# Feed-forward phases token-major, with the hidden halves turned by DMA, squares summed on ScalarE and low halves on VectorE

## The reference, cut to what matters

```python
x = x + 0.5 * ffn(layernorm(x), w_up, w_down)
x = x + attn(layernorm(x), Wq, Wk, Wv, Wo)      # also sums each 16 tokens of layernorm(x)
x = x + 0.5 * ffn(layernorm(x), w_up, w_down)

def ternary_linear(x, w):
    alpha = mean(abs(w)); w_t = sign(w) * (abs(w) > 0.5 * alpha)
    return einsum('bsd,fd->bsf', x / (rms(x) + 1e-8), w_t)
ffn(x) = ternary_linear(gelu(ternary_linear(x, w_up)), w_down)    # 256 -> 1024 -> 256
```

## Time and profile before

| | us |
|---|---|
| median of 3 runs | 2338.8 (2338.52 to 2339.14) |
| the profiled execution's own time | 2342.05 |
| its span, first to last instruction | 2340.3 |
| first feed-forward phase, first statistics to last side sum | 43.8 to 404.8 |
| attention | 404.8 to 2047.3 |
| second feed-forward phase, first statistics to end | 2047.6 to 2340.3 |

### The profile page before, as it was taken

How to read it: one execution, slowest core, us unless ns; L and a number is a source line. 1 busy time by engine, 2 the same in 40 slices (tenths; PEclk the granted TensorE clock), 3 DMA queues, 4 the chain that set the end, 5 groups by cost and what they waited for, 6 DMA issues and landing times. The chain is left out here.

```text
span 2340.3 us, 79203 instructions
## 1 busy us (share of the span) xinstructions
PE 2110.0 (90%) x30563; PEld 1603.8 (69%) x30563; DVE 1992.6 (85%) x4704; ACT 2050.7 (88%) x4166; POOL 1628.5 (70%) x1453
## 2 busy tenths in 40 slices
PE   1888885799999999999999999999999999879998
PEld 0555554578777777777777777777777777646666
DVE  6799996798888888898988988988889989768785
ACT  2888894599999989999998999998999999789997
POOL 1677775477777767777776777777677777556765
PEclk9999998899999999999999999999999999989999
DMA  5200000499999989999998999999999999801011
GB/s 180 72 0 0 0 0 1 76 170 167 173 171 167 175 135 171 168 176 168 171 169 140 171 171 172 173 171 161 150 169 173 170 168 178 128 10 36 27 36 37
DMA packets 1076094, 289.57 MB, mean 124 GB/s; under 512 B 1056304, under 2 KB 1074736, under 8 KB 1075760
## 3 DMA queue, kind: packets, MB, share of 16 engines
q1 hardware_dynamic: 1075760, 285.02, 77.1%
HBM read 14.68 MB, written 8.39 MB: 10 GB/s over the span
## 5 line engine op out<-in xcount | busy, mean ns | idle before, releaser
L1010 POOL TENSOR_TENSOR probs_split<-probs,probs_split 128x512 f16<-128x512 f32 (+1 forms) x1026 | 1148.5, 1131 | 429.3 <-DVE probs_split L1347 298.2
L1336 DVE CUSTOM_DVE_ANT_0 probs<-score_ps,mask,neg_qk_scale 128x512 f32<-128x512 f32 (+1 forms) x1028 | 740.5, 721 | 97.2 <-PE score_ps L1114 95.4
L1275 ACT ACTIVATE probs<-probs,minus_max 128x512 f32<-128x512 f32 (+1 forms) x1027 | 718.6, 700 | 90.4 <-DVE minus_max L1336 83.0
L1133 PEld LDWEIGHTS y_ps<-v_parts,probsT 128*128 128x128 f16 x11931 | 466.0, 98 | 90.3 <-DMA probsT<-probs_split 15.8
L1133 PE MATMUL y_ps<-v_parts,probsT 128*128 128x64 f16 x11931 | 515.4, 193 | 12.8 <-DMA probsT<-probs_split 11.7
L1290 ACT ACTIVATE probs_split<-probs 128x512 f16<-128x512 f32 (+1 forms) x770 | 471.3, 612 | 25.6 <-DMA probsT<-probs_split 11.4
L1111 PE MATMUL score_ps<-k_parts,q_parts 64*128 64x384 f16 (+3 forms) x2604 | 380.1, 286 | 19.8 <-DVE minus_max L1336 17.8
L1114 PE MATMUL score_ps<-k_parts,q_parts 64*128 64x384 f16 (+3 forms) x2604 | 380.1, 286 | 0.0
L1111 PEld LDWEIGHTS score_ps<-k_parts,q_parts 64*128 64x128 f16 x2604 | 196.4, 94 | 136.4 <-DVE minus_max L1336 45.1
L1043 PE MATMUL item_ps<-b_xT,wk_split 128*128 128x128 f16 x3168 | 222.2, 221 | 34.3 <-DVE b_xT L1328 32.3
L1043 PEld LDWEIGHTS item_ps<-b_xT,wk_split 128*128 128x128 f16 x3168 | 182.5, 98 | 57.1 <-DVE b_xT L1328 37.9
(11 more groups left out here) (174 smaller groups left out, 4112.7 us busy)
## 6 DMA issues: line engine op xcount, KB each, us to landing
probsT<-probs_split SPq DMA_TRANSPOSE x1031, 3.9
out_x<-x_resident SPq DMA_DIRECT2D x16, 512.0 KB, 2.9
x_resident<-in_L_attn_x SPq DMA_DIRECT2D x14, 512.0 KB, 4.4
raw_up<-in_L_ffn_w_up SPq DMA_DIRECT2D x1, 1024.0 KB, 5.7
raw_down<-in_L_ffn_w_down SPq DMA_DIRECT2D x1, 1024.0 KB, 7.6
raw_q<-in_L_attn_Wq SPq DMA_DIRECT2D x1, 1024.0 KB, 9.5
raw_k<-in_L_attn_Wk SPq DMA_DIRECT2D x1, 1024.0 KB, 11.5
raw_v<-in_L_attn_Wv SPq DMA_DIRECT2D x1, 1024.0 KB, 13.1
```

Of the source, the lines that this page charges most:

```text
L1010: nc.gpsimd.tensor_tensor(parts_of[ring(at, v)][:, LO, low_columns(place_of(at, v))], probs[v % NBUF][:, cols], parts_of[ring(at, v)][:, H ...
L1133: last = nc.tensor.matmul(out, pt[ring(at, v)][:, low * a + t, :], vr[:, slot, b, h * DH:(h + 1) * DH], start=(n == 0), stop=(n == len(pas ...
L1275: nc.scalar.activation(probs[v % NBUF][:, cols], probs[v % NBUF][:, cols], ACT.Exp, bias=bias[:, j % 2, h:h + 1], scale=-1.0, accum_out=su ...
L1336: nc.vector.tensor_tensor_reduce(out=probs[v % NBUF][:, cols], in0=score_ps[v % NBUF][:, cols], in1=mask_of(at, v), scale=w.neg_qk_scale[: ...
```

## The change

Every engine's program in `ffn_phase` is unrolled over 64 blocks, with no loop. `up` now holds 128 tokens as weights and streams 512 columns of w_up, so the hidden layer comes out token-major, [128 tokens, 1024 features], in two banks of each of two buffers. ScalarE runs one Gelu, one copy and one square of 128x1024 per block; the square has an accumulated output, which is the mean square of each token. VectorE makes the low half (GpSimd made it before). `down` needs features on partitions, so SP issues two DMA transposes for each block, high and low half, into rings of 4; `down` of a block comes three blocks behind its `up` (LAG). Loads and stores of x are single blocks of 128 KB. The side sums use float32 operands in place of halves. The reductions, the matrix of ones and the split of the second normalisation are gone.

```diff
+    LAG, RING_H = 3, 4
-        h = sb("h", [P, NF, TOK], F32)
-        hsq = sb("h_squared", [P, TOK, NF + 1], F32)
+        h = [sb(f"h{b}", [P, FF], F32) for b in range(2)]
+        h_parts = [[sb(f"h{s}{b}", [P, FF], F16) for b in range(RING_H)] for s in "hl"]
+        hT = [[sb(f"hT{s}{b}", [P, NF, P], F16) for b in range(RING_H)] for s in "hl"]
+        squares = sb("squares", [P, FF], F32)
+        h_ps = [psum(f"h_ps{b}", [P, FF]) for b in range(2)]
...
+            def turn_h(n, s, ready):
+                sp.wait_ge(ready, n + 1)
+                if n >= RING_H and s == HI:
+                    sp.wait_ge(down_done, n - RING_H + 1)
+                sp.dma_start_transpose(hT[s][n % RING_H][:], h_parts[s][n % RING_H][:]).then_inc(h_turned[s][n % RING_H], 16)
...
+            for n in range(NBLK):
+                turn_h(n, HI, hhi_ready)
+                turn_h(n, LO, hlo_ready)
+                if first and n + ahead < NBLK:
+                    load(n + ahead)
+                if out is not None and n >= 6:
+                    store(n - 6)
...
-            def h_lo(t, b, c):
-                nc.gpsimd.tensor_tensor(hs[LO][b][:, f], h[:, f], hs[HI][b][:, f],
+            rstd(0)
+            for t in range(NTILE + 1):
+                if t >= 1:
+                    hidden_rms(t - 1)
+                if t + 1 < NTILE:
+                    rstd(t + 1)
+                if first and t >= 1:
+                    rstd_second(t - 1)
...
-                nc.vector.tensor_reduce(hsq[:, :, NF], hsq[:, :, 0:NF // 2], AX_X, ALU.add).then_inc(half_summed, 1)
-                nc.vector.tensor_reduce(sqsum[:], hsq[:, :, NF // 2:], AX_X, ALU.add).then_inc(sqsum_ready, 1)
+            def h_lo(n):
+                dve.wait_ge(hhi_ready, n + 1)
+                if n >= RING_H:
+                    dve.wait_ge(h_turned[LO][n % RING_H], 16 * (n // RING_H))
+                nc.vector.tensor_tensor(h_parts[LO][n % RING_H][:], h[n % 2][:], h_parts[HI][n % RING_H][:],
+                                        ALU.subtract).then_inc(hlo_ready, 1)
...
+            for n in STEPS:
+                t, i = divmod(n, TB)
+                if i == 0:
+                    if more:
+                        normalise_begin(t + 1)
+                    if t < NTILE:
+                        x_lo(2 * t + 1)
+                    if first and t >= 3:
+                        side_split(t - 3)
+                if i == 1:
+                    if behind:
+                        output_scale(t - 1)
+                        add_output(TB * (t - 1))
+                        add_output(TB * (t - 1) + 1)
+                    if more:
+                        normalise_end(2 * (t + 1))
+                    if earlier:
+                        second_end(2 * (t - 2))
+                if i == 2:
+                    if more:
+                        normalise_end(2 * (t + 1) + 1)
+                    if earlier:
+                        second_end(2 * (t - 2) + 1)
+                if i == 3:
+                    if behind:
+                        add_output(TB * (t - 1) + 2)
+                        add_output(TB * (t - 1) + 3)
+                    if more:
+                        x_lo(2 * (t + 1))
+                    if first and behind:
+                        second_begin(t - 1)
+                if n < NBLK:
+                    h_lo(n)
...
+                            last = nc.tensor.matmul(h_ps[n % 2][:, f], xt[s][(n // 2) % 2][:, k, tok], w.w_up[:, k, f],
+                        last = nc.tensor.matmul(y_ps[:, n % TB], hT[s][n % RING_H][:, f], w.w_down[:, f],
+                        last = nc.tensor.matmul(g_ps[:, k, c * GPB:(c + 1) * GPB], xn2[half][:, c % 2, k * P:(k + 1) * P],
+                                                group32[:], start=True, stop=True)
...
+            for n in STEPS:
+                t, i = divmod(n, TB)
+                if n < NBLK:
+                    up(n)
+                if n == 0:
+                    turn(1)
+                if 0 <= n - LAG < NBLK:
+                    down(n - LAG)
+                if i >= 2 and t + 1 < NTILE:
+                    turn(2 * (t + 1) + i - 2)
+                if first and i >= 2 and 2 <= t < NTILE + 2:
+                    side(2 * (t - 2) + i - 2)
...
+                nc.scalar.activation(h[n % 2][:], h_ps[n % 2][:], ACT.Gelu).then_inc(gelu_done, 1)
+                nc.scalar.activation(h_parts[HI][n % RING_H][:], h[n % 2][:], ACT.Copy).then_inc(hhi_ready, 1)
+                nc.scalar.activation(squares[:], h[n % 2][:], ACT.Square, scale=2.0 * FF ** -0.5,
+                                     accum_out=ms[t % 2][:, c:c + 1]).then_inc(sq_done, 1)
```

More of the change, by code:

```diff
@@ new lines, in _ @@
+            ahead = PRELOADED * TB + 4
+            if first:
+                for n in range(PRELOADED * TB, ahead):
+                    load(n)
+            for n in range(NBLK):
[5 more added lines that the diff above has]
+                    store(n - 6)
+            if out is not None:
+                for n in range(NBLK - 6, NBLK):
+                    store(n)
+                sp.wait_ge(stored, 16 * NBLK)
@@ L387, in step @@
[L387 to L397, removed]
-                    rstd(t + 1)
[L399 to L414, removed]
@@ L429, in normalise_begin @@
[L429 to L433, removed]
+                dve.wait_ge(dve_step, done[0])
+            def normalise_begin(t):
+                if first and t >= PRELOADED:
+                    for n in range(TB * t, TB * t + TB):
+                        dve.wait_ge(x_loaded[n % 8], (n // 8) * 16)
                 for c in range(TB):
-                    last = nc.vector.bn_stats(stats[:, c], blk(t, c))
+                    last = nc.vector.bn_stats(stats[:, c], w.block(TB * t + c))
@@ L558, in _ @@
[L558 to L569 removed]
+            nc.vector.tensor_copy(group32[:], w.group16[:]).then_inc(group_ready, 1)
@@ new lines, in _ @@
+            normalise_begin(0)
+            normalise_end(0)
+            normalise_end(1)
+            x_lo(0)
+            for n in STEPS:
+                t, i = divmod(n, TB)
+                more = t + 1 < NTILE
+                behind = 1 <= t <= NTILE
+                earlier = first and 2 <= t < NTILE + 2
+                if i == 0:
[29 more added lines that the diff above has]
+                    h_lo(n)
@@ L591, in up @@
+            def up(n):
+                pe.wait_ge(xlo_ready, n // 2 + 1)
+                if n >= 2:
+                    pe.wait_ge(gelu_done, n - 1)
+                tok = slice((n % 2) * P, (n % 2) * P + P)
+                for half in range(2):
+                    f = slice(half * (FF // 2), (half + 1) * (FF // 2))
                     for k in range(KD):
                         for s in (HI, LO):
-                            last = nc.tensor.matmul(h_ps[f % 2][:], w.w_up[:, k, f * P:(f + 1) * P], xt[s][b][:, k],
-                                                    start=(n == 0), stop=(n == 2 * KD - 1))
@@ L650, in _, with down @@
-            tiles(pe, step)
+                            last = nc.tensor.matmul(h_ps[n % 2][:, f], xt[s][(n // 2) % 2][:, k, tok], w.w_up[:, k, f],
+                                                    start=(k == 0 and s == HI), stop=(k == KD - 1 and s == LO))
+                last.then_inc(up_done, 1)
+            def down(n):
+                if n >= TB:
+                    pe.wait_ge(y_added, n // 2 * 2 - TB + 2)
+                for s in (HI, LO):
+                    pe.wait_ge(h_turned[s][n % RING_H], 16 * (n // RING_H + 1))
+                    for f in range(NF):
+                        last = nc.tensor.matmul(y_ps[:, n % TB], hT[s][n % RING_H][:, f], w.w_down[:, f],
+                                                start=(s == HI and f == 0), stop=(s == LO and f == NF - 1))
+                last.then_inc(down_done, 1)
```

349 lines of the change are left out of this document (104 added, 245 removed).

## The result

| us | before | after |
|---|---|---|
| median of 4 runs | 2338.7 (2336.23 to 2339.14) | 2225.0 (2223.01 to 2227.52) |
| span of the profiled execution | 2340.3 | 2222.3 |
| first phase, first statistics to last side sum | 361.0 | 286.2 |
| attention with its ends | 1642.8 | 1639.9 |
| second phase, first statistics to end | 292.7 | 252.9 |

The change makes the kernel faster: the ratio is 0.9517, with an interval of 0.9500 to 0.9533. That is 113.7 us, where 78.8 were forecast. The median lies 1 us under the range's low end, close to rival (d), so the prediction was wrong in size, though not in sign, nor in the engine that it took as the bound.

A forecast was written before the change was run, and what follows sets the result against it. TensorE was taken to bound the second phase (15.4 us a tile), TensorE and VectorE jointly the first (17.1). Savings of 47 + 22 + 6 + 3 + 1 = 79 us took 2338.8 to 2260, range 2226 to 2300.

The forecast's parts named there:

- rival (d): Better packing: no TensorE pauses, side sums at 0.6, tiles 15.8 and 14.8; 108 us less, 2231; chance 15%.
- all starts and ends: Phase ends and prologues: 6 us less at the first phase's end, 3 at the second's, about 1 for prologues.
- The rows show a pause besides: TensorE, second phase: two pauses a tile, 0.6 us, kept on top of 14.8 us of work, giving 15.4.
- First phase: TensorE 17.2 (or 16.0) [...] I take 17.1: First-phase tile of 17.1 us, with float32 side sums at 1.8; 2.96 saved a tile, 47 us in all.
- Joined by waits both ways: First phase: TensorE at 17.2 (or 16.0) and VectorE at 15.8 to 16.5 wait for each other, tile 17.1.
- TensorE as the bound: Second phase: TensorE's 15.4 us a tile is the longest, with ScalarE 14.1 and DMA 13.9 below.
- 1.15 + 0.97 + 1.16: ScalarE per block: one Gelu, one copy, one square with accumulator read; 3.28 us, 14.1 a tile with x's copies.
- 0.7 us of blocking: VectorE, first phase: 15.8 us a tile becomes 16.5 if each GpSimd power blocks a normalisation once.
- rival (c): SP's queue: copies and transposes serialise, 6.0 us a block, 24 a tile; 176 us more, 2505; chance 6%.
- 15.4 - 13.9: TensorE's tile less DMA's: transposes 12.4 plus loads or stores 1.5 fit under 15.4, so cost nothing.
- Its limit of 1.9 us for a transpose: SP's queue: the transposes' cover under TensorE is gone if one takes over 1.9 us of the queue.
- four passes over 8 columns alone: Float32 side sums on TensorE: by the skill's four-pass rule, weight loads ignored, they would cost next to nothing; 1.8 was taken.

The follow-up runs named there:

- half of `down`: Changed kernel without the low halves' 8 `down` matmuls per block, transposes and waits kept: 2192.5 us, ratio 0.9388.

## Why the prediction was wrong in size

Measured as on record, by parts of the profiled span (118.0 us less; the median fell by 113.7, since the execution profiled before stood 3.4 above its median and the one after 0.6, and the time around the span grew from 1.75 to 3.3):

| | forecast | measured |
|---|---|---|
| second phase, 15.75 tiles | 22 (tile 15.4) | 35.7 (14.51) |
| first phase, 15.75 tiles | 47 (17.1) | 65.7 (15.89) |
| all starts and ends | 10 | 13.7 |
| attention | 0 | 2.9 |

- **The step that failed** is "The rows show a pause besides: 2163.51 to 2165.54 is 2.03 where 16 `down` matmuls need 1.75; two such pauses a tile make 0.6. I keep them, 15.4." The pause was taken as TensorE's own. It was a wait, and the trace of before says for what. The total waits between 2090 and 2320 us (total, times, longest), and two of them in the timeline, the second being the very pause that the prediction quotes, up to the `up` at 2165.54:
```profile
PEld h_ps_c L593 <- ACT h_c L667: 12.5, 25, 0.7
...
PEld y_ps_c L615 <- POOL hl_c L384: 5.7, 13, 0.5
```
```profile
2161.33 0.10 PEld L615 LDWEIGHTS y_ps_c<-w_down_ternary_T,hh_c 128*128 128x128 f16 x1 [0.42 <-POOL hl_c L384]
...
2165.53 0.10 PEld L593 LDWEIGHTS h_ps_c<-xTh_c,w_up_ternary_T 128*128 128x128 f16 x1 [0.40 <-ACT h_c L667]
```
  TensorE stood for ScalarE and for GpSimd's low halves, two things that the change takes away. Such a wait must be costed as gone once its cause has slack, unless a new one replaces it. After the change TensorE has no wait in 176 us. With the layout kept but ScalarE slowed (step of 9) it waits again, 1.7 us a tile, before its turns: a new wait in place of the old ones. This is 0.6 of the 0.89 a tile in the second phase. The rest, 0.2 to 0.3, is at the edges: three first steps without `down`, one last tile without turns; a tile within the phase takes 14.77, where the forecast without the pauses had 14.8.
- **The second miss** is "First phase: TensorE 17.2 (or 16.0) [...] I take 17.1", 1.2 too long. The pauses are half of it. The side sums were taken as 1.8 a tile and took 1.64, in 14 of the tiles alone: a step that runs two tiles late is absent between the first and the last low half of two tiles (28 x 0.82 / 15.75 = 1.46). "Joined by waits both ways" did not come: VectorE had 53.91 of 60, or 14.7 of the 16.4 us of a tile, for a forecast of 15.8 (its terms add up to 15.9).
- **TensorE as the bound**, the core of the forecast, holds: no idle time, and cutting its work cuts the tile (float16 side sums, half of `down`).
- **ScalarE.** Forecast 1.15 + 0.97 + 1.16. Gelu takes 1.02 us and 1.05 to the next start, the copy 0.97, square and read from start to start 1.04 (2051.55 to 2052.59). That is 3.06, not 3.28; ScalarE was further from being the bound than thought.
- **VectorE.** 1.23 us a low half for a forecast of 1.24, and GpSimd's powers did not touch the normalisations (406 ns), where the prediction allowed for 0.7 us of blocking.
- **DMA.** Landing was 3.2 us, the forecast had 3.9 to 6.1; issue 1.24 and 1.33 as forecast. Copies and transposes mixed in one queue don't serialise: rival (c) would have shown 24 us a tile. The slack under TensorE was forecast as 15.4 - 13.9 = 1.5 us and came out at 1.3 to 1.5, as both sides were smaller. Its limit of 1.9 us for a transpose left the copies out: (15.4 - 1.5) / 8 is 1.74.
- **Ends.** The last low half of the first phase starts 14.6 us before its last side sum (23.4 before), of the second 8.6 before the end (13.9); the second phase's start grew by 1.2. The 2.9 us of attention are scatter as far as the runs tell: in the eleven profiles of this document, which share its code, it lasts 1635 to 1645 us.
- **Rival (d)**, 2231, had the pauses gone, which is right. Its first phase of 15.8 comes near the measured 15.89 by luck: it took VectorE's sum, with side sums at 0.6, and it was TensorE, with side sums at 1.64. Its chance of 15% was too low, as the waits in the trace of before could have told.
- **What no run splits.** The contiguous square is worth 42 us, VectorE's low halves 12, and the float32 side sums cost 13. The other 70 or so of the 114 us go with the rest of the change (no reductions, no square sums, no loop), of which no part was run alone. In the second phase the loop can have cost 0.2 us a tile at most, as ScalarE was busy 16.69 of 16.90.

## What to carry to other kernels

Before an idle stretch of the engine that will be the new bound is carried into a forecast, look at what ended it: if the change removes the releaser and no new wait takes its place, the stretch goes too, and the floor is the sum of the engine's start-to-start times. A layout decides who pays for a reduction; look for the one in which the sum runs along a stream that an engine passes over anyway. Short operations that others wait for belong ahead of long ones in an in-order queue.

## What was not expected of the hardware

- Float32 matmuls of 8 columns take 0.10 us a record, almost the 0.11 of 128 columns. Their weight loads take 192 ns each in the changed kernel, where float16 ones take 96 to 98. So the price seems to be the weights, which no run separates, and narrow float32 products are dear: 13 us by the run that undoes them, where four passes over 8 columns alone, which the prediction weighed, would be next to nothing. The Trainium skill ("TensorE: Matmul & The Clock Gate", Weight-path perf modes) says that the fast weight load is off for float32 inputs; the trace agrees, with its 192 ns beside 96 to 98 (and 141 for the float32 transposes).
- VectorE and GpSimd hold each other up, and it matters which starts first. GpSimd's power of 4 elements a partition started 0.10 us before a low half of VectorE in the changed kernel and took 1.04 us; with float16 side sums it started 0.17 after one and took 1.95. The changed kernel has this by luck in 14 tiles of 16, and its one power of 1953 ns started behind a low half.
```profile
200.54 1.04 POOL L372 TENSOR_TENSOR rstd_a<-var_eps_a,pow_exp_a 128x4 f32<-128x4 f32 x1 [9.97 <-DVE var_eps_a L451]
200.64 1.23 DVE L427 TENSOR_TENSOR hl_a<-h_a,hh_a 128x1024 f16<-128x1024 f32 x1 [0.18 <-ACT hh_a L593]
```
```profile
212.47 1.96 POOL L374 TENSOR_TENSOR rstd_a<-var_eps_a,pow_exp_a 128x4 f32<-128x4 f32 x1 [2.37 <-DVE var_eps_a L463]
212.30 1.23 DVE L439 TENSOR_TENSOR hl_a<-h_a,hh_a 128x1024 f16<-128x1024 f32 x1
```
  The other way round, with GpSimd's low halves and the powers first, a normalisation that starts 0.30 us into one of them takes 1.99 us in place of 0.41 and ends 0.15 after it. Two and two:
```profile
201.12 4.27 POOL L378 TENSOR_TENSOR hl_a<-h_a,hh_a 128x1024 f16<-128x1024 f32 x2
201.42 4.13 DVE L428 TENSOR_SCALAR x_normed_a<-x_resident,mean_var_a,in_scale_a 128x256 f32<-128x256 f32 x2
```
- A strided read costs VectorE's reduction 1.6 times (2.82 to 4.61 us), a step of 9 costs ScalarE's write 2.0 times.
- Packed DMA transposes of 256 KB need 1.44 to 1.50 us each, with the DMA engines at 184 to 190 GB/s.
